# Turning quantised rows by DMA, and a freed PSUM bank for half of the gate products

## The reference

```python
def step(state, inp):
    d, b, c, u = inp
    dA = jnp.exp(d[..., None] * A)
    state = state * dA + (d * u)[..., None] * b[:, None, :]
    y = jnp.einsum('bdn,bn->bd', state, c)
    return (state, y)
...
def bitlinear(x, w):
    xn = rmsnorm(x)
    xq = xn + jax.lax.stop_gradient(activation_quant(xn) - xn)
    wq = w + jax.lax.stop_gradient(weight_quant(w) - w)
    return jnp.einsum('bsi,oi->bso', xq, wq)
h = jax.nn.silu(bitlinear(x, w1)) * bitlinear(x, w2)
return bitlinear(h, w3)
...
x = x + jnp.tanh(g_xattn[0]) * _L0_xattn_ref(ctx_1024, _layernorm(x, axis=-1), ...)
x = x + jnp.tanh(g_ffn[0]) * _L0_ffn_ref(_layernorm(x, axis=-1), L0_ffn_w1, L0_ffn_w2, L0_ffn_w3)
```

## Time and profile before

| | |
|---|---|
| median of 3 runs (lowest to highest) | 655.52 us (654.02 to 656.09) |
| the profiled execution, its time | 653.69 us |
| its span, first to last instruction | 651.9 us |
| mean granted TensorE clock | 0.897 |
| busy: POOL, DVE, ACT, PE | 587.9, 583.0, 530.7, 488.3 us |

### The profile page before, as it was taken

How to read it: one execution, slowest core, us unless ns; L and a number is a source line. 1 busy time by engine, 2 the same in 40 slices (tenths; PEclk the granted TensorE clock), 3 DMA queues, 4 the chain that set the end, 5 groups by cost and what they waited for, 6 DMA issues and landing times.

```text
span 651.9 us, 7928 instructions
## 1 busy us (share of the span) xinstructions
PE 488.3 (75%) x2560; PEld 296.4 (45%) x2560; DVE 583.0 (89%) x772; ACT 530.7 (81%) x969; POOL 587.9 (90%) x289
## 2 busy tenths in 40 slices
PE   8798878994564678777666486778676887668987
PEld 3254434552553445455534354455454554345543
DVE  6779779997998899999999999989997999999765
ACT  5764767788999778987798797899999898897675
POOL 1399999998999999999999999999999999999431
PEclk9988999997555979999786889889989897978999
DMA  5598587579960100147420100037700000000001
GB/s 186 193 407 309 183 329 276 198 270 389 374 262 0 39 1 2 47 153 276 132 78 0 33 2 17 1 127 244 254 37 1 17 1 18 0 16 18 1 17 48
DMA packets 24472, 80.77 MB, mean 124 GB/s; under 512 B 2464, under 2 KB 5152, under 8 KB 21360
## 3 DMA queue, kind: packets, MB, share of 16 engines
q1 hardware_dynamic: 24432, 80.27, 33.9%
HBM read 72.53 MB, written 7.73 MB: 123 GB/s over the span
## 4 chain that ended last, share of the span: by engine, by line
POOL 30%; DVE 29%; ACT 14%; issue 13%; PE 11%; DMA 2%; SPq 0%; DVEq 0%; POOLq 0%; ACTq 0%
POOL hh L708 15%; POOL hh L818 14%; DVE hh L773 9%; DVE hh L770 8%; DVE room L1048 4%; ACT da L736 3%; DVE sm L1093 2%; PE bank_a L1020 2%; PE bank_b L1029 2%; PE bank_y L851 2%; ACT room L1041 1%; PE da L1211 1%; DVE bank_y L576 1%; DVE sm L904 1%; ACT gbuf L922 1%
## 5 line engine op out<-in xcount | busy, mean ns | idle before, releaser
L773 DVE TENSOR_TENSOR_SCAN hh<-da,hh 128x1024 f32<-128x1024 f32 x85 | 193.4, 2280 | 3.1 <-ACT da L743 3.0
L851 PE MATMUL bank_y<-ident,hh 128*128 128x128 f32 x1024 | 145.3, 292 | 10.8 <-POOL hh L818 8.8
L851 PEld LDWEIGHTS bank_y<-ident,hh 128*128 128x128 f32 x1024 | 129.6, 152 | 40.1 <-issue 17.5
L813 POOL TENSOR_TENSOR hh<-hh,cc 128x1024 f32<-128x1024 f32 x60 | 141.0, 2350 | 0.2 <-ACT hl L756 0.2
L818 POOL TENSOR_TENSOR hh<-hh,cc 128x1024 f32<-128x1024 f32 x57 | 134.2, 2355 | 0.0
L708 POOL TENSOR_TENSOR hh<-pair,bb 128x1024 f32<-128x1024 f32 x30 | 70.5, 2352 | 26.4 <-DMA bb<-xd_scratch 24.2
L770 DVE TENSOR_TENSOR_SCAN hh<-da,hl,hh 128x256 f32<-128x256 f32 x128 | 85.4, 729 | 0.0
L708 POOL TENSOR_TENSOR hh<-wq,bb 128x1024 f32<-128x1024 f32 x32 | 75.3, 2357 | 1.8 <-PE bank_y L851 1.8
L702 POOL TENSOR_TENSOR hh<-wq,bb 128x1024 f32<-128x1024 f32 x32 | 75.1, 2346 | 0.3 <-PE bank_y L851 0.3
L702 POOL TENSOR_TENSOR hh<-pair,bb 128x1024 f32<-128x1024 f32 x32 | 75.2, 2355 | 0.0
L736 ACT ACTIVATE da<-wq,cst 128x256 f32<-128x256 f32 x128 | 53.3, 463 | 12.0 <-DVE hh L770 11.6
(11 more groups left out here) (271 smaller groups left out, 1051.7 us busy)
## 6 DMA issues: line engine op xcount, KB each, us to landing
bb<-xd_scratch SPq DMA_DIRECT2D x32, 512.0 KB, 5.1
cc<-xd_scratch SPq DMA_DIRECT2D x32, 512.0 KB, 6.9
wq<-weights SPq DMA_DIRECT2D x12, 1024.0 KB, 6.5
stage<-weights SPq DMA_DIRECT2D x8, 1024.0 KB, 6.1
xin<-x SPq DMA_DIRECT2D x4, 1024.0 KB, 5.4
room<-weights SPq DMA_DIRECT2D x4, 1024.0 KB, 8.2
u_scratch<-wq SPq DMA_DIRECT2D x6, 512.0 KB, 3.0
wq<-x SPq DMA_DIRECT2D x2, 1024.0 KB, 18.8
```

Source lines behind the costliest of these rows:

```text
L773: ins = v.tensor_tensor_scan(to, da, h, 0.0, ALU.mult, ALU.add)
L813: ins = g_.tensor_tensor(quarters(flat(hh[k % NH])), quarters(flat(hh[k % NH])), cc[:, n:n + 4, t], ALU.mult)
L851: mm = pe.matmul(bank_y[:, (first + c) * P:(first + c + 1) * P], flat(hh[k % NH])[:, at:at + P], ident[:, :], start=False, stop=(s == STEP ...
```

## The change

For tiles 0 to 11 (`by_dma`) the 16 transposes of h on PE and both evictions on ACT go. In their place SP issues two DMA transposes per tile, in slot 8, each of one half (128 x 1024 16-bit values), from the rounded rows straight into `hqT`. They carry the shift of 1536 along, which the evictions took off; so PE, once, in slot 36, makes the sums of w3 over its rows (16 matmuls with a column of ones, into `bank_t`), ACT copies them to SBUF, and each output product begins with a matmul of one row that subtracts 1536 times the sums. Since `bank_t` is no longer needed for h, a of chunks 1 and 3 of these tiles goes there, so that it waits for the g of two chunks earlier; `out_tensor` in turn waits for the last g of the next tile and for the transposes' landing. Tiles 12 to 15 keep the old way.

```diff
+SUMS = 36
...
+        ones16 = sb("ones16", [P, 1], F16)
...
+        hqT16 = view(room, 5120, 1024).bitcast(F16).rearrange("p (a b) -> p a b", a=KF)
+        w3sum = view(room, 6400, 256).bitcast(F16)[0:1, :]
+        offset = ones[0:1, 0:P // 2].bitcast(F16)
...
+        def column_sums(pe):
+            pe.wait_ge(*WA.of(("sign", NW - 1)))
+            pe.wait_ge(*YV.of(("p", NE - 1)))
+            pe.wait_ge(*PV.of("ident16"))
+            for f in range(KF):
+                mm = pe.matmul(bank_t[0:1, :], ones16[:, :], w3q[:, f, :], start=(f == 0), stop=(f == KF - 1))
+            WP.did(mm, "columns")
+        def column_sums_scalar(act):
+            act.wait_ge(*WP.of("columns"))
+            WA.did(act.activation(w3sum, bank_t[0:1, :], ACT.Copy), "columns")
...
+            WV.did(v.memset(offset, -MAGIC16), "offset")
...
         def bank_ab(i, c):
+            if by_dma(i) and c % 2:
+                return bank_t, bank_b
...
+        def by_dma(i):
+            return i < END - 1
...
             elif i == 0:
-                pe.wait_ge(*x_done(i))
-                pe.wait_ge(*PV.of("ident16"))
+                pe.wait_ge(*WA.of("columns"))
...
+        def a_before(i, c):
+            if by_dma(i):
+                return (i, c - 2) if c >= 2 else (i - 1, 2) if c == 0 else None
+            return chunk_before(i, c)
         def a_tensor(pe, i, c):
-            a, before = bank_ab(i, c)[0], chunk_before(i, c)
+            a, before = bank_ab(i, c)[0], a_before(i, c)
+            if by_dma(i) and c == 1:
+                j = max(j for j in range(NE, 4 * NE) if z_turn_slot(j) < tile_slot(i) + 1)
+                pe.wait_ge(*ZA.of(("gT", j)))
...
+        def turn_by_dma(sp, i):
+            for r in range(2):
+                sp.wait_ge(*MA.of(("hq", i, r)))
+                if r == 0 and i:
+                    sp.wait_ge(*MP.of(("o", i - 1)))
+                d_turn[r].did(sp.dma_start_transpose(hqT16[:, 8 * r:8 * r + 8, :], h16_at(i, r)), ("hqT", i, r))
...
         def out_tensor(pe, i, groups=range(NCH)):
-            if i < END - 1:
-                pe.wait_ge(*MA.of(("hqT", i, 1)))
+            if by_dma(i) and 0 in groups:
+                pe.wait_ge(*ZA.of(("gT", max(j for j in range(NE, 4 * NE) if z_turn_slot(j) < turned(i) + 2))))
+                if tile_slot(i + 1) - 1 < turned(i) + 2:
+                    pe.wait_ge(*MA.of(("xqT", i + 1)))
+                    if by_dma(i + 1):
+                        pe.wait_ge(*MV.of(("g", i + 1, NCH - 1)))
+                pe.wait_ge(*WV.of("offset"))
+                pe.matmul(bank_g(i)[:, :], offset, w3sum, start=True, stop=False)
             for g in groups:
+                if by_dma(i):
+                    pe.wait_ge(*d_turn[g // 2].of(("hqT", i, g // 2)))
...
+                        if k == turned(i):
+                            turn_by_dma(sp, i)
...
+                    if k == SUMS:
+                        column_sums_scalar(act)
...
-                    for i in range(END - 1):
-                        if k == tile_slot(i) + 9:
-                            hqt_scalar(act, i, 1)
-                    for i in range(END - 1):
-                        if k == tile_slot(i) + 8:
-                            hqt_scalar(act, i, 0)
...
+                    if k == SUMS:
+                        column_sums(pe)
...
-                    for i in range(END - 1):
-                        if k == tile_slot(i) + 9:
-                            ht_tensor(pe, i, 1)
-                    for i in range(END - 1):
-                        if k == tile_slot(i) + 8:
-                            ht_tensor(pe, i, 0)
...
+                v.memset(ones16[:, :], 1.0)
```

## The result

The changed kernel takes 666.01 us in the median of 4 runs (663.6 to 666.31), the kernel before 655.63 in 4 runs: ratio 1.0155, interval 1.0125 to 1.0184. It is slower, as forecast, but by 10.4 us and not by 3.1. The profiled execution is the shortest of the four, 663.6 us (span 661.7).

What follows compares the result with a forecast made beforehand. POOL was taken as the bound. A 3.4 us stall from the column sums less 0.3 us gained gave +3.1 us: 656.8 us for the profiled execution, 658.6 for the median, range 654.0 to 666.

Steps and rivals of the forecast that it cites:

- What bounds the kernel: In the loop, 217 to 606 us, POOL is busy without a break; at most about 0.3 us can be won.
- what the removal is worth: Tiles 0 to 11: taking 16 transposes per tile off PE and 26 us off ACT booked at 0.
- PE gets past its chunk no sooner: Odd chunks: b still waits for h of the chunk before; 0.2 to 0.3 us per odd chunk, booked at 0.
- The column sums: Slot 36: 16 matmuls on PE, 5.26 us, delay ACT's rounding and tanh; POOL stalls 3.4 us at step 57.
- The transposes hidden: DMA transposes of h land in 2 to 5 us each, within 11 us of room: cost 0.
- The output product's wait for the last gated value: Output product, each tile: waits for the next tile's last gated value, 1.0 us later at tile 0, booked at 0.
- the stall of the loop is the largest of the single lags, not their sum: Whole loop: once POOL is 3.4 us late, the output product's 1.0 us lag adds nothing.
- Transposes late: Rival, 12 tiles: transposes outlast the 11 us and delay the output product; +72 us, 727 us, at 14 us landing 670; chance 0.14.
- No change: Rival, slot 36: column sums at full clock, 3.62 us, +1.5, 657.0 us, or hidden, 655.5; chance 0.28.
- faster: Rival, slots 39 to 124: POOL's products partly waiting, DVE the bound; 2 to 5 us less, 652 us; chance 0.08.

Runs made afterwards that it cites:

- both losses undone: Changed kernel with a in one bank again and the column sums made early, transposes and offset matmul kept: 654.84 us, ratio 0.9993 against the kernel before.
- one bank: Changed kernel with a of every chunk in bank_a again, transposes, late column sums and offset matmul kept: 659.39 us, ratio 1.0063 against the kernel before.
- the sums early: Changed kernel with the column sums in four parts in slots 35 and 36, in bank_b, shared bank kept: 661.61 us, ratio 1.0089 against the kernel before.
- the filler: Early column sums with the shared bank, plus eight unread matmuls on PE before the offset matmul: 661.49 us, ratio 1.0099 against the kernel before.

## Where the prediction was right and where it went wrong

- **What bounds the kernel, and what the removal is worth: right.** With both losses undone, 26 us less on ACT and 16 transposes less per tile give a ratio of 0.9993. That POOL alone is the bound was too simple, though: with 4.7 us taken off it (and 2.4 put on DVE), it waits for PE's sums, and the time stays. A second chain, through DVE and PE, stands close behind, or comes close by that load.
- **PE gets past its chunk no sooner: right.** The wait went from a to b, 49.1 to 54.2 us.
- **The column sums: mechanism right, place and size somewhat off.** PE 5.28 us (5.26 forecast), the rounding 4.69 late (4.9), the tanh 3.62 (4.1), POOL's waits 3.68 (3.4). They came at steps 53 and 54, though, not at step 57 with its 0.1 us of room: behind the late gated value PE had stood idle for 3.14 us, and the sums that step 53 needs took 1.91 us in place of 1.04. The medians make the term 4.4 to 4.6. That PE's time came out to 0.02 us is luck: the granted clock was 0.50 up to 206 us and 1.00 from 207 on, while in the profile of one bank it stayed at 0.50 up to 209 us, the sums took 6.15 us, and POOL's waits up to step 57 came to 4.4. So the sums' price differs from one execution to the next, and the changed kernel's profile is that of its shortest.
- **The transposes hidden: right.** They land in 3.2 us, at most 6.1. The rule of the Trainium skill that spoke against this, "VectorE: DVE Perf Modes", section The three transpose paths, gives 1309 ns per 128 x 128 block, 10.5 us (an estimate) for the 8 blocks of one transfer one after another; the trace does not agree. The Trainium skill's other page, "Advanced Engine Details and Errata", section X-Bar Transpose (TRN2), by which a transposing DMA is as fast as an ordinary one, is nearer, but 3.2 us stand against 2.1 for a store of as many bytes.
- **The output product's wait for the last gated value: the step that failed.** It was sized at 1.0 us from tile 0 and booked at 0, because "the stall of the loop is the largest of the single lags, not their sum". It cost 6.6 to 6.8 us. Two things were wrong in it. First, the two do add: the wait costs 6.8 us with the sums early and 6.6 with them late. The forecast had it that a late POOL gives every engine more room; the likely reason why not, argued and not measured, is that the sums' lag moves DVE along with POOL, so that the gated value, on which the output product now hangs, is as late as POOL is. Second, the size was read off one tile. Up to slot 79 DVE's program has g ahead of the gate, as in tile 0, but from slot 80 on behind it. In slots 80 and 104 DVE works without a break through the scan, the gate and the addition of x behind it, and only then makes g, while PE waits 2.78 and 2.50 us; the output product behind took 5.3 us in place of 3.62. Putting g ahead of the gate gave back 5.6 and 4.8 us. In other slots PE waits as well (2.35 us in slot 60, with a scan and a product by C ahead of g); in all, 4 of the 12 products took 5.3 to 5.4 us, against one of 5.26 before. The prediction asked what is queued behind the waiting instruction, but not what is queued on DVE ahead of the one that is waited for.
- **The rivals.** Transposes late: fell. (Its price is too high as well: it counts from 256.05 us, which stands in no row; by the earlier trace rows the second half is first read at 255.17 + 1.8 = 256.97, so a landing at 264.1 is 7.1 and not 8 us late, and the price some 61 us, not 72.) No change, faster: fell. What decided was no rival at all, but a term that had been set to 0.
- **The range.** The measured time lies at its upper end, 666, and that end was put there for late transposes, which did not come. That the range reaches so far is luck.

Open: how much of the bank's cost is the clock and how much the order on DVE. The order is worth 4.8 to 5.6 us by the medians, the filler nothing, but each edit also changes how long PE stands idle.

## What to carry to other kernels

A buffer that is freed and then shared with a later reader moves its wait to another instruction: look up what stands in the queue ahead of the new releaser, in every slot where the two meet, and not in one of them. Do not count on a lag in one stage to hide a lag in another: here the two added, with no idle time on the bound engine between them. In this loop, where POOL was busy without a break, taking work off PE and ACT was worth nothing, while 9.2 us of new waits of POOL made 9.9 us between the profiled executions.

## What was new about the hardware

A transposing DMA of 128 x 1024 16-bit values within SBUF landed in 3.2 us in the median, and SP needed about 1.3 us to issue one, against 0.3 for a store. Each was cut into some 1050 packets (49816 in all against 24472, the new ones under 512 bytes), and the 512 KB loads of bb landed in 6.6 us in place of 5.1 in the median. None of it cost time: with both losses undone and the transposes still there, bb landed in 6.4 us and the ratio was 0.9993. And the granted clock, in the busy time by stretch around slot 104 of the changed kernel:

```profile
513.00:517.00 4.00, 1.50 (x10) 0.77 (x9) 3.83 (x6) 2.80 (x7) 4.00 (x3) 0.98 0.00 0
517.00:522.00 5.00, 5.00 (x19) 2.23 (x18) 3.12 (x3) 4.89 (x12) 3.14 (x2) 0.67 0.00 2
```

PE, busy for 1.50 of 4.00 us, is granted 0.98 while it waits and 0.67 on the mean once it works without a break: the lower level fell on the work behind the idle time, 5.31 us of output product in place of 3.62. It does not always: behind 2.35 us of idle time in slot 60 of the same execution the product ran at the full clock.

```profile
313.12 0.37 PE L1240 MATMUL bank_t<-room,ones 1*128 1x512 f16 x1 [2.35 <-DVE room L1082]
313.43 3.63 PE L1249 MATMUL bank_t<-wq,room 128*128 128x512 fp8e4 x16
```
